# The first stage in one block, and the norm of each stack ahead of its constants

## The chip, the cores and the metric

The kernel runs on one core of a Trainium2 chip. The metric is the device time of one execution in microseconds (us). The kernel before took 4556.93 us, the median of three runs (4550.22 to 4557.34).

A core has five engines with an instruction stream each: TensorE (PE), VectorE (DVE), ScalarE (ACT), GpSimd (POOL) and SyncE (SP). They meet through semaphores. [...]

## What is computed

Input x is 2 x 1024 x 128 in float32. Four parts follow each other, each adding to x what it makes of a normalised x:

```python
x = x + attn_a(layernorm(x))     # 16 heads of 8, causal over 1024 tokens, full softmax
x = x + stack(layernorm(x))      # 6 layers: windowed attention (16 heads of 64, window 32), then a gated FFN;
                                 # ahead of each of the two, half of the features shift by one token
x = x + attn_b(rmsnorm(x))       # gated slot attention, 4 heads of 32, a scan over the tokens
x = x + stack(layernorm(x))      # the same six layers' worth again
```

Only the first part and the entry of the two stacks matter for the change. In the first part q, k and v are projections of the normalised x with a bias, the scores are `q k^T / sqrt(128)` below the diagonal, and the softmax of them weighs v.

## The kernel before

Everything is kept feature-major: `xT` is 128 features by 2048 tokens, cut into NC = 4 chunks of 512 tokens. Each part is one or more blocks. At the end of a block all engines meet, and the next block's instructions begin on all of them together.

*Loading (block 1).* SP loads two identities, the matrix `jmean` and x (1 MB, tokens on the partitions) into `xtok`. TensorE turns it into banks 0 to 3, ScalarE copies the banks into `xT`, VectorE sets three small constants.

*First stage, block 2.* SP loads the four weights and biases and two masks. GpSimd blanks the packing buffers and fills the padded values: `qp`, `kp` (twice, zeros and then rows of ones), `nmz`, `vz`, and counts each in `blank_set`, to 7 (lines 331 to 340). TensorE, ScalarE and VectorE run the layer norm, a chain over the four chunks: product with jmean, centring, square, product with jmean, logarithm, exponential, multiplication (`ln_pe`, `ln_act`, `ln_dve`, lines 111 to 145). When all is normalised (`norm_done`), TensorE transposes the weights, ScalarE copies them into `wT`, and the twelve projections follow, q, k and v of each chunk, through six banks. Since float32 products are made of a high and a low part here, ScalarE copies a projection rounded to its high part (`qhi`, `khi`, line 378), and VectorE makes the low part from the bank (`qlo`, `klo`, line 391); ScalarE copies v into `vz` (line 381). ScalarE waits for `blank_set` 7 ahead of all twelve copies.

*First stage, block 3.* The scores of a pair of heads need their rows packed: the 8 rows of a head are copied by DMA four times under each other (high, low, high, low for q; high, high, low, low for k). That is 16 DMAs of 32 KB for a pair (`pack`, line 409), in six slots. SP issues those of q for all 16 pairs and those of k from pair 3 on; ScalarE those of k for pairs 0 to 2 (EARLY). TensorE then runs through a hand-written order (`turns`, lines up to 300): 12 score pieces of a pair, each reduced to a negative maximum by VectorE (line 571), then the maxima packed in, and from the 15th step on the turned scores with ScalarE's exponentials, GpSimd's masks and the products with the values beside them. The stretch up to the first exponential is called the fill below.

*Stack entry.* SP issues the constants (`rot` of 2 MB, `band`, `head_of`, `take`, `minus_hi`, line 707), four small scales (line 710), and then eight pairs of weights (lines 714 and 717). TensorE waits for all five constants (`const_ld`) and then runs the norm. VectorE waits for GpSimd's zeroing (`zeroed`, lines 791 to 794) and for the constants, copies `take` (line 1063), runs the norm, and copies `y` with the shift into `xs`, two copies a chunk (line 1070). The first step of the loop waits for `take_set`, for the first chunk of `xs` and for the weights of all eight pairs.

Of the kernel before, what the change touches and what calls it, by code (L numbers as in the profile page):

```python
# [5 lines left out]
F32 = mybir.dt.float32  # L6
BF16 = mybir.dt.bfloat16
F32R = mybir.dt.float32r
# [65 lines left out]
def hybrid_kernel(nc, w, c, out):  # L74
# [10 lines left out]
    with ctx:  # L85
# [61 lines left out]

# [6 lines left out]
        with ExitStack() as inner:  # L154
            scope[0] = inner
            xtok = sb("xtok", [P, N // P, D])
            with nc.Block() as block:
                @block.sync
                def _(sp):
                    for n, (dst, src) in enumerate(((ident[:, :], c["ident"]), (identb[:, :], c["identb"]),  # L160
                                                    (jmean[:, :], c["jmean"]))):
                        sp.dma_start(dst, src).then_inc(const_ld, 16)
                    sp.dma_start(xtok[:, :, :], w["L0_attn_a_x"].rearrange("b (n p) d -> p (b n) d", p=P))\
                        .then_inc(x_ld, 16)

                @block.tensor
                def _(pe):
                    pe.wait_ge(const_ld, 48)
                    pe.wait_ge(x_ld, 16)
                    for k in range(NC):  # L170
                        for i in range(4):
                            m = pe.transpose(bank[k][:, i * P:(i + 1) * P], xtok[:, 4 * k + i, :], ident[:, :])
                        m.then_inc(tin_mm, 1)

                @block.scalar
                def _(act):
                    for k in range(NC):
                        act.wait_ge(tin_mm, k + 1)
                        act.activation(xT[:, cs(k)], bank[k][:, :], ACT.Copy).then_inc(tin_cp, 1)

                @block.vector
                def _(dve):
                    dve.memset(ln_eps[:, :], LN_EPS).then_inc(eps_set, 1)
                    dve.memset(ss_eps[:, :], SS_EPS).then_inc(eps_set, 1)
                    dve.memset(ss_back[:, :], SS_BACK).then_inc(eps_set, 1)
            scope[0] = ctx


        stage_a(nc, w, c, sem, bank, wide, xT, y, ident, identb, ln_pe, ln_act, ln_dve, cs, 0, cen, sqr, rstd)
# [39 lines left out]
def stage_a(nc, w, c, sem, bank, wide, xT, y, ident, identb, ln_pe, ln_act, ln_dve, cs, ln_call, cen, sqr, rstd):  # L229

    PP = HA // 2
# [52 lines left out]
    with ExitStack() as st:  # L284
# [24 lines left out]
        norm_done = sem("a_normed")  # L309
# [8 lines left out]

        with nc.Block() as block:
            @block.sync  # L320
            def _(sp):
                for i, nm in enumerate("qkvo"):
                    sp.dma_start(wtok[:, i, :], w[f"L0_attn_a_W{nm}_w"]).then_inc(a_ld, 16)
                    sp.dma_start(bias[:, i:i + 1], w[f"L0_attn_a_W{nm}_b"].rearrange("(p a) -> p a", a=1))\
                        .then_inc(a_ld, 16)
                for dst, src in ((rowm[:, :], c["a_rowm"]), (dmask[:, :], c["a_dmask"])):
                    sp.dma_start(dst, src).then_inc(a_ld, 16)

            @block.gpsimd
            def _(pool):  # L330
                pool.memset(qp[:, :, :].bitcast(F32), 0.0).then_inc(blank_set, 1)
                pool.memset(kp[:, :, :].bitcast(F32), 0.0).then_inc(blank_set, 1)
                pool.wait_ge(blank_set, 2)
                for e in range(2):
                    pool.memset(kp[64 * e + NMAX:64 * e + NLOW + 1, :, :].bitcast(F32), 1.0).then_inc(blank_set, 1)
                    pool.wait_ge(blank_set, 3 + e)
                pool.memset(nmz[:, :, :, :], 0.0).then_inc(blank_set, 1)
                pool.memset(vz[:, :, :, :], 0.0).then_inc(blank_set, 1)
                pool.wait_ge(blank_set, 6)
                pool.memset(vz[:, :, :, VONE:VONE + 1], 1.0).then_inc(blank_set, 1)  # L340

            @block.tensor
            def _(pe):
                ln_pe(pe, ln_call, lambda k: xT[:, cs(k)])
                pe.wait_ge(a_ld, 16 * 10)
                pe.wait_ge(norm_done, 1)
                for i in range(4):
                    m = pe.transpose(bank[0][:, i * P:(i + 1) * P], wtok[:, i, :], ident[:, :])
                m.then_inc(wt_mm, 1)
                pe.wait_ge(wt_cp, 1)  # L350
                for k in range(NC):
                    for i in range(3):
                        n = 3 * k + i
                        o = pbank(n)
                        if n >= 6:
                            if i < 2:
                                pe.wait_ge(lo_cp, 2 * (k - 2) + i + 1)
                            else:
                                pe.wait_ge(v_cp, k - 1)
                        if i < 2:  # L360
                            m = pe.matmul(o, wT[:, i, :], hT(k), start=True, stop=True)
                        else:
                            for t in range(4):
                                m = pe.matmul(o[:, t * P:(t + 1) * P], y[:, (4 * k + t) * P:(4 * k + t + 1) * P],
                                              wT[:, 2, :], start=(t == 0), stop=(t == 3), skip_group_check=True)
                        m.then_inc(pr_mm, 1)

            @block.scalar
            def _(act):
                ln_act(act, ln_call)  # L370
                act.wait_ge(wt_mm, 1)
                act.activation(wT[:, :, :], bank[0][:, :].rearrange("p (i d) -> p i d", i=4), ACT.Copy).then_inc(wt_cp, 1)
                act.wait_ge(blank_set, 7)
                for n in range(3 * NC):
                    k, i = divmod(n, 3)
                    act.wait_ge(pr_mm, n + 1)
                    if i < 2:
                        act.activation((qhi, khi)[i][:, k, :].bitcast(F32R), pbank(n), ACT.Identity, bias=bias[:, i:i + 1])\
                            .then_inc(hi_cp, 1)
                    else:  # L380
                        act.activation(vz[:, 4 * k:4 * k + 4, :, 0:HD],
                                       pbank(n).rearrange("p (t h r) -> p t h r", t=4, r=HD), ACT.Copy).then_inc(v_cp, 1)

            @block.vector
            def _(dve):
                ln_dve(dve, ln_call, lambda k: xT[:, cs(k)], hT)
                dve.drain().then_inc(norm_done, 1)
                for k in range(NC):
                    for i in range(2):
                        dve.wait_ge(hi_cp, 2 * k + i + 1)  # L390
                        dve.scalar_tensor_tensor(out=(qlo, klo)[i][:, k, :].bitcast(F32R), in0=pbank(3 * k + i),
                                                 scalar=bias[:, i:i + 1], in1=(qhi, khi)[i][:, k, :],
                                                 op0=ALU.add, op1=ALU.subtract).then_inc(lo_cp, 1)
# [24 lines left out]
        with nc.Block() as block:  # L418
            @block.sync
            def _(sp):  # L420
                sp.wait_ge(blank_set, 4)
# [13 lines left out]
            def _(pe):  # L435
                def turned_scores(x, e):
# [87 lines left out]
            def _(act):  # L524
                def oz_copy(act, x):
# [8 lines left out]
                act.wait_ge(blank_set, 4)  # L534
                act.wait_ge(lo_cp, 4)
                for p in range(EARLY):
                    pack(act, p, kp, (khi, khi, klo, klo))
# [1389 lines left out]
```

## Time and profile before

| | us |
|---|---|
| median of three runs | 4556.93 |
| lowest, highest | 4550.22, 4557.34 |
| the profiled execution | 4552.66 |
| its span in the trace | 4550.9 |

The profile is one execution. Its first part gives for each engine the busy time, its share of the span and the count of instructions. A row of the busy table by stretch has the window (us from the span's start) and its length, then for PE, PEld (weight loads), DVE, ACT and POOL the busy us with the count in brackets, then the granted clock of TensorE as a share of full speed (1.00 is 2.4 GHz, 0.50 is 1.2 GHz, values between are a mean of the two over the window), then the share of the DMA engines that was busy, and GB/s. A row of the timeline has start, duration, engine, line and operation, output <- input with shapes, a count of merged instructions, and in brackets the idle time of the engine before it and what ended it. SPq and ACTq are the issuing queues; the duration of a DMA there is the time to issue it, not to move its bytes.

### The profile page before, as it was taken

Reading aid. Unit: us, or ns where it says so; the run is one execution under the profiler, and the core shown is the slowest. Engines: PE = TensorE matmul, PEld = TensorE weight load, DVE = VectorE, ACT = ScalarE, POOL = GpSimd, SP = SyncE. Lnnn points to the kernel's source line nnn. Section 1 sums busy time; section 2 is a strip of 40 time slices with the busy share of each in tenths; the row PEclk is TensorE's granted clock in tenths of the full one; section 3 lists DMA queues with packets and bytes.
Section 4 is the critical chain, followed back from the end, with each engine's and each line's share of the span. In section 5 each row is a group of like instructions: output and inputs, shape, how many; then the busy total and the mean of one; then the engine's idle time right before and its main releaser. Section 6 shows DMA issues by size and latency. Waiting matters only on the chain. (4 is left out here: it accounts for less than half of the span.)

```text
span 4550.9 us, 115940 instructions
## 1 busy us (share of the span) xinstructions
PE 4202.9 (92%) x44625; PEld 2515.2 (55%) x44625; DVE 3453.2 (76%) x4977; ACT 3069.5 (67%) x7028; POOL 1809.8 (40%) x1075
## 2 busy tenths in 40 slices
PE   5997999999999999999857579999999999999996
PEld 3443556555656555556526445656556556655653
DVE  4773888888888888888625468888888888888883
ACT  2554777777777777777652257777777777777774
POOL 2111444444444444444314524444444444444442
PEclk7997999999999999999976589999999999999998
DMA  2112444444443444444200044444434444444331
GB/s 41 28 22 63 95 106 99 104 96 97 104 105 88 110 98 100 97 100 97 61 10 3 3 104 107 101 92 105 104 89 104 97 103 103 93 104 105 91 91 36
DMA packets 239314, 382.03 MB, mean 84 GB/s; under 512 B 65636, under 2 KB 128736, under 8 KB 238472
## 3 DMA queue, kind: packets, MB, share of 16 engines
q1 hardware_dynamic: 238344, 373.28, 35.6%
q8 instruction: 386, 6.32, 0.6%
q10 hardware_dynamic: 384, 0.79, 0.1%
q14 instruction: 200, 1.64, 0.1%
HBM read 39.22 MB, written 1.05 MB: 9 GB/s over the span
## 5 line engine op out<-in xcount | busy, mean ns | idle before, releaser
L801 POOL TENSOR_TENSOR b_prob<-b_prob,b_rinv 128x768 f32<-128x768 f32 x384 | 564.2, 1469 | 1897.6 <-DVE b_rinv L1135 1897.6
L807 POOL TENSOR_TENSOR b_prc<-b_prc,b_sws 128x1024 f32<-128x1024 f32 x384 | 905.8, 2359 | 80.6 <-DMA b_sws<-b_prs 80.6
L1050 ACT ACTIVATE b_prob<-ps,b_nmx 128x96 f32<-128x96 f32 x3072 | 748.8, 362 | 0.0
L845 PEld LDWEIGHTS ps<-ident,b_prob 128*128 128x128 f32 x3072 | 378.8, 141 | 416.2 <-issue 300.9
L1076 DVE SCALAR_TENSOR_TENSOR b_prc<-ps,b_qks,b_rot 128x512 f32<-128x512 f32 x768 | 570.3, 743 | 9.6 <-ACT b_sq L1013 8.7
L1078 DVE SCALAR_TENSOR_TENSOR b_prs<-ps,b_qks,b_rot 128x512 f32<-128x512 f32 x768 | 569.1, 741 | 0.0
L1116 DVE TENSOR_TENSOR b_prc<-b_prc,ps 128x512 f32<-128x512 f32 x384 | 263.4, 686 | 386.3 <-PE ps L901 326.4
L1033 ACT ACTIVATE b_oT<-ps 128x512 f32<-128x512 f32 x384 | 226.9, 591 | 359.5 <-PE ps L859 359.5
L845 PE MATMUL ps<-ident,b_prob 128*128 128x128 f32 x3072 | 464.3, 274 | 2.9 <-ACT b_pT L988 2.9
L1089 DVE SCALAR_TENSOR_TENSOR b_rsp<-b_rhi,b_minus_hi,b_rn 128x512 fp32r<-128x512 f32 x192 | 376.9, 1963 | 114.7 <-ACT b_rn L999 114.7
L936 PE MATMUL ps<-b_wqkv,b_xs 128*128 128x128 f32 x3072 | 446.5, 289 | 1.8 <-DVE b_prs L1078 1.6
L988 ACT ACTIVATE b_pT<-ps 128x512 f32<-128x512 f32 x724 | 436.4, 603 | 10.3 <-PE ps L845 10.2
L859 PE MATMUL ps<-b_pT,b_vs 128*64 128x64 f32 x6144 | 436.8, 234 | 0.3
L890 PE MATMUL ps<-b_xs,b_wqkv 128*128 128x512 f32 x768 | 406.0, 610 | 22.4 <-ACT b_va L1038 8.3
L950 PE MATMUL ps<-b_oT,b_wo 128*128 128x512 f32 x768 | 412.4, 619 | 5.6 <-ACT b_oT L1033 5.6
L859 PE MATMUL ps<-b_pT,b_va 128*64 128x64 f32 x6144 | 399.7, 222 | 0.0
L906 PE MATMUL ps<-b_xs,b_wqkv 128*128 128x512 f32 x768 | 397.3, 599 | 0.5
L936 PEld LDWEIGHTS ps<-b_wqkv,b_xs 128*128 128x128 f32 x3072 | 373.3, 192 | 32.6 <-issue 6.9
L1140 DVE TENSOR_REDUCE b_nmx<-ps 128x8 f32<-128x768 f32 x384 | 353.2, 920 | 48.1 <-PE ps L925 47.6
L859 PEld LDWEIGHTS ps<-b_pT,b_vs 128*64 128x64 f32 x6144 | 307.7, 136 | 110.7 <-issue 64.5
L1132 DVE TENSOR_REDUCE b_ssm<-b_prob 128x8 f32<-128x768 f32 x384 | 361.5, 941 | 0.0
L1026 ACT ACTIVATE b_sq<-ps 128x512 f32<-128x512 f32 x384 | 229.4, 597 | 183.3 <-PE ps L906 182.9
(252 smaller groups left out, 7283.8 us busy)
## 6 DMA issues: line engine op xcount, KB each, us to landing
b_sws<-b_prs SPq DMA_DIRECT2D x1536, 128.0 KB, 2.3
b_vs<-b_va SPq DMA_DIRECT2D x768, 128.0 KB, 2.4
b_wqkv<-in_L_ffn_Wqkv SPq DMA_DIRECT2D x96, 192.0 KB, 2.9
b_xs<-y SPq DMA_DIRECT2D x132, 128.0 KB, 2.4
b_wo<-in_L_ffn_Wo SPq DMA_DIRECT2D x96, 64.0 KB, 2.2
b_xs<-y SPq DMA_DIRECT2D x44, 127.8 KB, 2.4
b_rot<-in_rot SPq DMA_DIRECT2D x2, 2048.0 KB, 7.7
b_w<-in_L_ffn_W SPq DMA_DIRECT2D x24, 170.5 KB
```

The costliest lines, as they stand in the source:

```text
L801: pool.tensor_tensor(prob[:, r, :, P - KEYS:P], prob[:, r, :, P - KEYS:P], rinv[:, r % 2, :].rearrange("p (b a) -> p b a", a=1).broadcast_ ...
L807: pool.tensor_tensor(prc[:, r, :, :], prc[:, r, :, :], sws[:, r % 2, :, :], ALU.add)\
L845: t = pe.transpose(bank[6][:, i * P:(i + 1) * P], prob[:, kd, 4 * e + 2 * h + m, :], ident[:, :])
L859: t = pe.matmul(bank[7][es, n * BLK:(n + 1) * BLK], v[:, es], pT[:, h, 2 * e + m, o * BLK:(o + 1) * BLK], start=(n == 0), stop=(n == NB - ...
L890: pe.matmul(bank[0][:, :], W[:, 0, :], X, start=True, stop=True).then_inc(S["q_mm"], 1)
L906: pe.matmul(bank[1][:, :], W[:, 1, :], X, start=True, stop=True).then_inc(S["k_mm"], 1)
L936: m = pe.matmul(bank[0][:, t * P:(t + 1) * P], xs[:, at:at + P], W[:, 2, :], start=(t == 0), stop=(t == 3), skip_group_check=True)
L950: pe.matmul(bank[3][:, :], wo[:, pair(d), :], oT[:, kd % 2, :], start=True, stop=True).then_inc(S["wo_mm"], 1)
L988: act.activation(pT[:, h, :, :], bank[6].rearrange("p (i q) -> p i q", i=4), ACT.Copy)\
L1050: g = act.activation(prob[:, kb, i, P - KEYS:P], wide[0][:, e * CH + m * KEYS:e * CH + (m + 1) * KEYS], ACT.Exp, bias=nmx[:, kb % 2, i:i + 1])
L1076: dve.scalar_tensor_tensor(out=prc[:, r, i, :], in0=bank[i][:, :], scalar=scale, in1=rot[:, 2 * i, t], op0=ALU.mult, op1=ALU.mult)
L1078: dve.scalar_tensor_tensor(out=prs[:, r % 2, i, :], in0=bank[i][:, :], scalar=scale, in1=rot[:, 2 * i + 1, t], op0=ALU.mult, op1=ALU.mult) ...
```

## The change

1. Blocks 1 to 3 become one block. `xtok` is no longer a buffer of its own but a view of `y`. The copies into `xT` and the products with jmean are coupled by `tin_cp` chunk by chunk. GpSimd's blanking stands at the start of its stream.
2. TensorE transposes the weights when the last chunk is centred (`cen_done`), no longer after the last normalised chunk; each chunk's projections wait for that chunk's `norm_done`.
3. On ScalarE only the copy of the first v waits for `blank_set` 7. Its order is: copies of chunks 0 and 1, key DMAs of pair 0, copies of chunks 2 and 3, key DMAs of pairs 1 and 2. Before, all copies came first.
4. TensorE waits for all low parts and all copies of v (`lo_cp`, `v_cp`) ahead of its first score.
5. In a stack TensorE runs the norm ahead of its wait for the constants. VectorE too, and it copies each chunk with the shift right behind that chunk's norm (`each`); the copy of `take` comes behind the norm. SP issues the weights of the first pair (FIRST) ahead of the constants, and the others behind the scales; the first two steps of the loop wait for the first pair's weights alone.

The core of the diff:

```diff
-        def ln_dve(dve, n, src, dst, gain=None):
+        def ln_dve(dve, n, src, dst, gain=None, each=None):
...
+                    if each:
+                        dve.wait_ge(norm_done, NC * n + i + 1)
+                        each(i)
...
+        xtok = y[:, :].rearrange("p (n d) -> p n d", d=D)
...
+        def x_ready(pe, k):
+            pe.wait_ge(tin_cp, k + 1)
...
             @block.tensor
             def _(pe):
-                ln_pe(pe, ln_call, lambda k: xT[:, cs(k)])
+                x_turns(pe)
+                ln_pe(pe, ln_call, lambda k: xT[:, cs(k)], x_ready)
                 pe.wait_ge(a_ld, 16 * 10)
-                pe.wait_ge(norm_done, 1)
+                pe.wait_ge(cen_done, NC)
...
                 for k in range(NC):
+                    pe.wait_ge(norm_done, k + 1)
+                    if k == 1:
+                        pe.wait_ge(lnv_done, NC)
...
+                pe.wait_ge(lo_cp, 2 * NC)
+                pe.wait_ge(v_cp, NC)
...
             @block.scalar
             def _(act):
+                x_copies(act)
+                ln_act(act, ln_call)
...
+                        else:
+                            if k == 0:
+                                act.wait_ge(blank_set, 7)
...
+                def keys(p):
+                    act.wait_ge(lo_cp, 4)
+                    pack(act, p, kp, (khi, khi, klo, klo))
+
+                projections(0)
+                projections(1)
+                keys(0)
+                projections(2)
+                projections(3)
+                for p in range(1, EARLY):
+                    keys(p)
...
+        FIRST = 1
...
+                for p in range(FIRST):
+                    load_qkv(0, p)
+                    load_wo(0, p)
                 for dst, src in ((rot[:, :, :], c["rot"]), (band[:, :, :], c["band"]), (head_of[:, :], c["head_of"]),
...
-                for p in range(PAIRS):
+                sp.wait_ge(S["wqkv_ld"], ONE + 16 * (PAIRS * L0 + FIRST))
+                for p in range(FIRST, PAIRS):
                     load_qkv(0, p)
                     load_wo(0, p)
...
+                ln_pe(pe, ln_call, lambda k: xT[:, cs(k)])
                 pe.wait_ge(S["const_ld"], ONE + 80 * (rep + 1))
-                ln_pe(pe, ln_call, lambda k: xT[:, cs(k)])
                 pe.wait_ge(S["take_set"], ONE + rep + 1)
...
-                            pe.wait_ge(S["wqkv_ld"], ONE + 16 * PAIRS * (L0 + 1))
+                            pe.wait_ge(S["wqkv_ld"], ONE + 16 * (PAIRS * L0 + (FIRST if j < 2 * FIRST else PAIRS)))
...
-                dve.wait_ge(S["zeroed"], ONE + ZERO * (rep + 1))
+                def shift(k, dve=dve):
+                    if k == 0:
+                        dve.wait_ge(S["zeroed"], ONE + ZERO * (rep + 1))
+                    for to, frm in shifted(k):
+                        dve.tensor_copy(to, frm).then_inc(S["xin_done"], 16)
+
+                ln_dve(dve, ln_call, lambda k: xT[:, cs(k)], lambda k: y[:, cs(k)], each=shift)
                 dve.wait_ge(S["const_ld"], ONE + 80 * (rep + 1))
```

## Rows read from the trace of the kernel before

**Rows 1.** The page's first part: busy time, share and instructions of each engine.

```profile
PE 4202.9 (92%) x44625; PEld 2515.2 (55%) x44625; DVE 3453.2 (76%) x4977; ACT 3069.5 (67%) x7028; POOL 1809.8 (40%) x1075
```

**Rows 2.** Busy time by stretch: the fill, and the start of each stack.

```profile
60.00:100.00 40.00, 27.61 (x112) 13.82 (x112) 27.62 (x35) 0.00 (x0) 0.00 (x0) 0.50 0.41 58
...
400.00:405.00 5.00, 0.00 (x0) 0.00 (x0) 0.44 (x1) 1.28 (x1) 0.00 (x0) 0.72 0.65 215
...
2620.00:2625.00 5.00, 2.81 (x6) 0.91 (x4) 2.29 (x4) 1.18 (x1) 1.18 (x5) 0.92 0.12 23
```

**Rows 3.** The timeline from 0 to 54 us, all engines.

```profile
0.90 0.06 DVE L183 MEMSET ln_eps<- 128x1 f32 x1 [0.90 <-PEq L1916]
...
13.59 5.22 POOL L331 MEMSET a_qp<- 128x6144 f32 x1 [13.05 <-POOLq L157]
...
25.44 0.60 ACT L372 ACTIVATE a_wT<-ps 128x512 f32<-128x512 f32 x1 [1.58 <-PE ps L348]
...
32.20 1.05 PE L364 MATMUL ps<-a_wT,y 128*128 128x128 f32 x8
...
43.29 0.52 POOL L340 MEMSET a_vz<- 128x256 f32 x1
43.85 0.69 ACT L378 ACTIVATE cen<-ps,a_bias 128x512 fp32r<-128x512 f32 x1 [17.81 <-POOL a_vz L340]
...
46.62 0.62 ACT L381 ACTIVATE a_vz<-ps 128x512 f32<-128x512 f32 x1
46.88 0.74 DVE L391 SCALAR_TENSOR_TENSOR a_klo<-ps,a_bias,rstd 128x512 fp32r<-128x512 f32 x1
...
53.28 0.75 DVE L391 SCALAR_TENSOR_TENSOR a_klo<-ps,a_bias,rstd 128x512 fp32r<-128x512 f32 x1
```

**Rows 4.** The timeline from 54 to 96 us: key DMAs, first score of pairs 0 to 2.

```profile
54.38 1.90 ACTq L409 DMA_DIRECT2D a_kp<-rstd  x2
...
62.75 2.30 ACTq L409 DMA_DIRECT2D a_kp<-rstd  x2
...
66.69 0.47 PE L477 MATMUL ps<-a_kp,a_qp 64*128 64x128 f32 x2 [13.28 <-DMA a_kp<-a_klo]
...
79.14 0.47 PE L477 MATMUL ps<-a_kp,a_qp 64*128 64x128 f32 x2
...
94.19 0.47 PE L477 MATMUL ps<-a_kp,a_qp 64*128 64x128 f32 x2
```

**Rows 5.** The timeline of the first stack's entry, 400 to 425 us.

```profile
400.72 0.34 SPq L707 DMA_DIRECT2D b_rot<-in_rot  x1
...
407.50 0.13 POOL L794 MEMSET b_xs<- 64x1 f32 x2
...
410.96 3.78 PE L115 MATMUL ps<-xT,jmean 128*128 128x512 f32 x4 [11.84 <-DMA b_minus_hi<-in_minus_hi]
411.00 0.43 DVE L1063 CAST b_take<-b_prs 128x512 fp32r<-128x512 f32 x1 [10.56 <-DMA b_minus_hi<-in_minus_hi]
...
417.76 0.68 DVE L143 TENSOR_TENSOR y<-cen,rstd 128x512 f32<-128x512 f32 x1
...
418.87 0.69 DVE L138 TENSOR_TENSOR cen<-xT,ps 128x512 f32<-128x512 f32 x1 [0.43 <-PE ps L115]
...
422.86 0.69 DVE L143 TENSOR_TENSOR y<-cen,rstd 128x512 f32<-128x512 f32 x1 [0.64 <-ACT rstd L130]
423.64 3.59 DVE L1070 COPY b_xs<-y 64x512 f32<-64x512 f32 x8
...
424.77 2.04 PE L890 MATMUL ps<-b_xs,b_wqkv 128*128 128x512 f32 x2 [3.33 <-DVE b_xs L1070]
```

**Rows 6.** The timeline of the second stack's entry, 2623 to 2648 us.

```profile
2623.80 0.33 SPq L707 DMA_DIRECT2D b_rot<-in_rot  x1
...
2634.17 3.78 PE L115 MATMUL ps<-xT,jmean 128*128 128x512 f32 x4 [11.36 <-DMA b_minus_hi<-in_minus_hi]
...
2647.43 1.33 PE L890 MATMUL ps<-b_xs,b_wqkv 128*128 128x512 f32 x2 [3.34 <-DVE b_xs L1070]
```

More of the change, by code:

```diff
@@ L151, in hybrid_kernel @@
         eps_set = sem("eps_set")
[L154 to L186, printed above, removed]
@@ new lines, in x_copies, with eps_values @@
+        def x_copies(act):
+            for k in range(NC):
+                act.wait_ge(tin_mm, k + 1)
+                act.activation(xT[:, cs(k)], bank[k][:, :], ACT.Copy).then_inc(tin_cp, 1)
+            act.wait_ge(eps_set, 3)
+        def eps_values(dve):
+            dve.memset(ln_eps[:, :], LN_EPS).then_inc(eps_set, 1)
+            dve.memset(ss_eps[:, :], SS_EPS).then_inc(eps_set, 1)
+            dve.memset(ss_back[:, :], SS_BACK).then_inc(eps_set, 1)
+        def x_ready(pe, k):
+            pe.wait_ge(tin_cp, k + 1)
@@ L435, in _ @@
             def _(pe):
+                x_turns(pe)
+                ln_pe(pe, ln_call, lambda k: xT[:, cs(k)], x_ready)
+                pe.wait_ge(a_ld, 16 * 10)
+                pe.wait_ge(cen_done, NC)
+                for i in range(4):
+                    m = pe.transpose(bank[0][:, i * P:(i + 1) * P], wtok[:, i, :], ident[:, :])
+                m.then_inc(wt_mm, 1)
+                pe.wait_ge(wt_cp, 1)
+                for k in range(NC):
+                    pe.wait_ge(norm_done, k + 1)
+                    if k == 1:
+                        pe.wait_ge(lnv_done, NC)
+                    for i in range(3):
+                        n = 3 * k + i
+                        o = pbank(n)
+                        if n >= 6:
+                            if i < 2:
+                                pe.wait_ge(lo_cp, 2 * (k - 2) + i + 1)
+                            else:
+                                pe.wait_ge(v_cp, k - 1)
+                        if i < 2:
+                            m = pe.matmul(o, wT[:, i, :], hT(k), start=True, stop=True)
+                        else:
+                            for t in range(4):
+                                m = pe.matmul(o[:, t * P:(t + 1) * P], y[:, (4 * k + t) * P:(4 * k + t + 1) * P],
+                                              wT[:, 2, :], start=(t == 0), stop=(t == 3), skip_group_check=True)
+                        m.then_inc(pr_mm, 1)
+                pe.wait_ge(lo_cp, 2 * NC)
+                pe.wait_ge(v_cp, NC)
                 def turned_scores(x, e):
@@ L524, in _, with projections @@
             def _(act):
+                x_copies(act)
+                ln_act(act, ln_call)
+                act.wait_ge(wt_mm, 1)
+                act.activation(wT[:, :, :], bank[0][:, :].rearrange("p (i d) -> p i d", i=4), ACT.Copy).then_inc(wt_cp, 1)
+                def projections(k):
+                    for i in range(3):
+                        n = 3 * k + i
+                        act.wait_ge(pr_mm, n + 1)
+                        if i < 2:
+                            act.activation((qhi, khi)[i][:, k, :].bitcast(F32R), pbank(n), ACT.Identity, bias=bias[:, i:i + 1])\
+                                .then_inc(hi_cp, 1)
+                        else:
+                            if k == 0:
+                                act.wait_ge(blank_set, 7)
+                            act.activation(vz[:, 4 * k:4 * k + 4, :, 0:HD],
+                                           pbank(n).rearrange("p (t h r) -> p t h r", t=4, r=HD), ACT.Copy).then_inc(v_cp, 1)
+                def keys(p):
[8 more added lines that the diff above has]
+                    keys(p)
                 def oz_copy(act, x):
@@ L532, in oz_copy @@
                                 act.activation(oz[:, c_, :], bank[3][:, :], ACT.Copy).then_inc(oz_cp, 1)
[L534 to L537, printed above, removed]
                 for x in range(LAST):
@@ L552, in _ @@
             def _(pool):
+                pool.memset(qp[:, :, :].bitcast(F32), 0.0).then_inc(blank_set, 1)
+                pool.memset(kp[:, :, :].bitcast(F32), 0.0).then_inc(blank_set, 1)
+                pool.wait_ge(blank_set, 2)
+                for e in range(2):
+                    pool.memset(kp[64 * e + NMAX:64 * e + NLOW + 1, :, :].bitcast(F32), 1.0).then_inc(blank_set, 1)
+                    pool.wait_ge(blank_set, 3 + e)
+                pool.memset(nmz[:, :, :, :], 0.0).then_inc(blank_set, 1)
+                pool.memset(vz[:, :, :, :], 0.0).then_inc(blank_set, 1)
+                pool.wait_ge(blank_set, 6)
+                pool.memset(vz[:, :, :, VONE:VONE + 1], 1.0).then_inc(blank_set, 1)
                 zero = pool.to_reg(0.0)
@@ L561, in _ @@
             def _(dve):
+                eps_values(dve)
+                ln_dve(dve, ln_call, lambda k: xT[:, cs(k)], hT)
+                for k in range(NC):
+                    for i in range(2):
+                        dve.wait_ge(hi_cp, 2 * k + i + 1)
+                        dve.scalar_tensor_tensor(out=(qlo, klo)[i][:, k, :].bitcast(F32R), in0=pbank(3 * k + i),
+                                                 scalar=bias[:, i:i + 1], in1=(qhi, khi)[i][:, k, :],
+                                                 op0=ALU.add, op1=ALU.subtract).then_inc(lo_cp, 1)
+                dve.wait_ge(blank_set, 7)
                 for g in range(GS):
```

110 lines of the change are left out of this document (29 added, 81 removed).

## The prediction, made before the change was run

> **What bounds the kernel now.** The page's busy shares come first: TensorE is busy for 92% of the span [rows 1]. A change that leaves TensorE's work alone can therefore only gain where TensorE stands still, so the next view is the table of busy time by stretch. The change touches no line inside the long loops of the two stacks, so the stretches to look at are the front of the first stage and the two stack entries: from 60 to 100 us TensorE has 27.61 us of work in 40 us, at a granted clock of 0.50, and ScalarE has none [rows 2]. The timeline of these places is read third, and the reader is to look at the bracket behind each row: it says what ended the idle time.
>
> In the first stage two waits follow each other. GpSimd starts its blanking memsets only when the second block starts, at 13.59, and ends them at 43.81 (43.29 + 0.52), a run of 30.2 us; ScalarE's copies of the projections wait 17.81 us for that [rows 3]. When the last low part is made (53.28 + 0.75 = 54.03), a block ends, and the packing DMAs begin at 54.38. The first score waits for them until 66.69, idle for 13.28 us [rows 3, 4]. At each stack entry the norm, which needs nothing but xT, waits for the constants: the block starts at 400.72 and the first mean product at 410.96; in the second stack it is 2623.80 and 2634.17, and from there to the first projection 13.8 and 13.3 us pass [rows 5, 6].
>
> **The first stage, part by part.** *Blanking.* The memsets move to the start of the program. The other engines' first instructions stand at 0.90 there [rows 3], so the run ends at 0.9 + 30.2 = 31.1. No memset is added. GpSimd's later masks are far behind (their first exponentials come after the fill), so nothing waits behind the move.
>
> *Projections of chunks 0 and 1.* In the trace of before the last product of chunk 1 ends at 32.20 + 1.05 = 33.25 [rows 3]. The weight transposes now don't wait for the last norm but for the last centred chunk, so at least the 1.58 us go that ScalarE stood idle before its copy of the weights at 25.44 [rows 3]: 31.7 at most. q0 and k0 are copied under the memsets. The copy of v0 keeps its wait and starts at 31.1. Copies started back to back come every 0.57 us (six from 43.85 to 47.24, rows 3): q1 at 31.7, k1 at 32.3, v1 at 32.85, ended at 33.5. VectorE's low part of k1 starts 0.83 us after its copy (46.88 against 46.05, which is 46.62 less one step) and takes 0.74: 33.85 [rows 3]. Then both queues may pack pair 0, at 33.9 instead of 54.38: 20.5 us earlier.
>
> *Pair 0 and the projections of chunks 2 and 3.* This is the new order, and the one place where the change adds a wait. ScalarE's queue issues the 8 key DMAs of pair 0 first, and these took from 54.38 to 62.75, 8.4 us (1.05 us each) [rows 4]. Behind them on ScalarE stand the six copies of chunks 2 and 3; behind these the lower parts on VectorE; and TensorE now waits for all of those ahead of its first score. ScalarE is free at 33.9 + 8.4 = 42.3, the fifth copy (k3) starts at 42.3 + 4 x 0.57 = 44.6, its low part ends 0.83 + 0.75 later at 46.2. The other arm is the landing: from the start of packing to the first score it took 66.69 - 54.38 = 12.3 us [rows 4], which gives 33.9 + 12.3 = 46.2. Both arms end together, and the first score starts at about 46.2 instead of 66.69: **-20.5 us**. Whichever arm is late costs one for one. TensorE's own products for chunks 2 and 3 run beside ScalarE's issuing from 32 on and hide.
>
> *Pairs 1 and 2.* Before, the keys of pair 1 were issued from 62.75 and the first score of pair 1 stood at 79.14, 12.4 us behind the first of pair 0 [rows 4]. Now they are issued from 45.7, take 8.4, and land 3.9 later (66.69 against 62.75, rows 4), at 58.0. They are wanted at 46.2 + 12.4 = 58.6, so 0.6 us are to spare. Pair 2 is issued until 62.5, lands at 66.4, and is wanted at 94.19 - 20.5 = 73.7 [rows 4]. SP's own packing begins 20.5 us earlier like everything else and keeps its lead. The fill is a chain of products and reductions that does not change, so the 20.5 us arrive at the stage's end. Bounds: -22 if landing and copies both come a little early; if an issue came a third dearer, at 1.4 us instead of 1.05, 2.8 us would be lost in each of pairs 0 and 1, less the 0.6 to spare, so -15.5.
>
> The Trainium skill ("DMA: Bandwidth & Descriptors", Issuing engines are not separate DMA queues) says that DMAs of ScalarE and SP run on the same 16 engines and interleave, and that a second issuer saves only issue time. By that rule a pause of ScalarE's issuing lets SP run ahead and loses no transfer time, and pair 1 would land earlier than I count; no run here shows it yet.
>
> **The stack entries.** The first mean product needs only xT and may start with the block, at about 400.95. That moves the norm by 10.0 us. From its first mean product to the last normalised chunk it took 410.96 to 423.55 [rows 5]. Into VectorE's part of it come the shift copies, 3.59 us for eight, or 0.9 us for a chunk [rows 5]. Chunk 0: y at 407.76, ended 408.44, copies to 409.4. GpSimd's zeroing, for which they wait, ends at 407.50 + 0.13, just in time. The fourth centring stood at 418.87, would be at 408.87, and comes at 409.4, so 0.55 us late, and the last y with it: 422.86 - 10.0 + 0.55 = 413.4. It ends at 414.1, its copies at 415.0. Then the copy of take, which was ahead of the norm and is now behind it, 0.43 us [rows 5]: 415.45. The first projection starts at 415.5 instead of 424.77: **-9.3 us**.
>
> Of the queue: SP issues the first weights ahead of the constants, two more DMAs, and its remaining 14 behind the scales as before. The constants landed 10.2 us after the block's start (410.96, rows 5); with a tenth more bytes ahead of them (by the shapes 256 KB, beside 2 MB of rot and 0.5 MB of the others) and two more issues that becomes some 11.5 to 12, against the 14.7 us at which they are now wanted. I cost it at nothing; the cover is 3 us. The weights of the other pairs are wanted by the third slot only.
>
> The clock: a stack's block starts with a granted clock that is not yet at its lower level (0.72 over 400 to 405, 0.92 over 2620 to 2625, rows 2), while the norm of before started at the lower one. The first four records of mean products took 3.78 us at the lower one [rows 5]; at twice the clock some 1 us of that goes ahead of the first centring. In stack 0 the zeroing at 407.63 holds the copies, which caps the gain at -10.0. In stack 1 nothing does: up to -10.5. I take **-9.7** and **-10.0**; the ends are -9.3 and -10.0, and -9.4 and -10.5. The loops behind are unchanged and start earlier by as much.
>
> **The sum.** 20.5 + 9.7 + 10.0 = 40.2 us. The profiled execution took 4552.66, so its like would take 4512.5; the median of the three runs is 4556.93, and two of them stand at 4557, which gives 4516.7. I predict **4515**. Terms at their ends give -34 to -43.
>
> **The rivals.** *Late keys* (A): ScalarE's issuing is slower than before or pair 1 lands late, because SP competes for the whole time. For it: the two arms are level and only 0.6 us are to spare. Against: SP competed before too. It gives back 5 to 10 us: about 4523.
>
> *Constants bind again* (B): they land after 14.7 us, or the early weights delay them, and the norm's lead turns into a new wait on the same constants. Half of the stacks' 19.7 is lost: about 4525. It is also the form in which the change wouldn't do what it says.
>
> *Warm fill* (C): the fill of before ran wholly at 0.50 [rows 2], after 13.28 us of idle TensorE [rows 4]; now the idle stretch in front is some 8 us. Were it warm, TensorE's 27.61 us there would be about half, and since VectorE's reductions (27.62 us of these 40, rows 2) are then the limit, some 5 us more go: about 4510. The Trainium skill ("TensorE: Matmul & The Clock Gate", What's actually happening) says that the low clock is the default and that activity releases it; by that rule the fill, unchanged in density, stays cold and C fails.
>
> *Slower* (D): ScalarE issues become much dearer, since the keys now sit between its copies. Price with 3.6 us an issue: the first score at 33.9 + 28.8 + 3.9 = 66.6, pair 1 at 33.9 + 28.8 + 3.4 + 28.8 + 3.9 = 98.8, pair 2 at 127.6, where it was wanted at 94.19 before [rows 4]. That is 33 us late less 19.7 from the stacks: 4570. It decides from some 3.3 us an issue on, and the trace shows 1.05 [rows 4].
>
> **How the numbers follow.** Forecast (-34 to -43) 0.60; A 0.15; B 0.09; C 0.08; D 0.03; the shift is absorbed later, within 9 us of no change, 0.04; left over 0.01. The range reaches over A, B and C and takes in the 7 us between the runs shown: 4504 to 4532. Chances: faster by over 0.2% (about what a measurement of this kernel can tell from no change, 9 us) 0.93, same 0.04, slower 0.03.
>
> **What would show it.** After: the last blanking memset ends near 31; ScalarE's first key DMA at 34; first score at 46, released by a DMA or by VectorE's last low part; pair 1's first score without a wait for a DMA; in each stack the first mean product with the block's first instructions and the first projection 14.5 to 15 us later, released by VectorE's copy of take. A wait of the take copy for minus_hi would be B, a wait of pair 1's score for a DMA would be A. The prediction is wrong if the fill is longer than 34 us or if the loops' own pace changes.

## The result and the profile after

| | before | after |
|---|---|---|
| median of four runs | 4557.14 | 4510.53 |
| lowest, highest | 4550.22, 4560.46 | 4507.91, 4520.66 |
| the profiled execution | 4552.66 | 4512.50 |

The ratio is 0.991, with a 95% interval of 0.9894 to 0.9926: 34 to 48 us less. The forecast was 4515, in a range of 4504 to 4532. Between the two profiled executions lie 40.2 us, which is what the sum gave; between the medians lie 46.6. Single runs of one kernel here differ by ten us and more, so both agree with the sum.

The front of the changed kernel, in the timeline (start, duration, engine, line, operation, in brackets the idle time before it and its releaser):

```profile
0.83 5.22 POOL L541 MEMSET a_qp<- 128x6144 f32 x1 [0.29 <-POOLq L1933]
...
30.53 0.53 POOL L550 MEMSET a_vz<- 128x256 f32 x1
31.16 0.60 ACT L502 ACTIVATE a_vz<-ps 128x512 f32<-128x512 f32 x1 [4.52 <-PE ps L389]
...
33.80 1.90 ACTq L333 DMA_DIRECT2D a_kp<-rstd  x2
...
42.18 0.69 ACT L497 ACTIVATE cen<-ps,a_bias 128x512 fp32r<-128x512 f32 x1 [8.78 <-issue]
42.35 1.07 ACTq L333 DMA_DIRECT2D a_kp<-rstd  x1
...
45.21 0.74 DVE L566 SCALAR_TENSOR_TENSOR a_klo<-ps,a_bias,rstd 128x512 fp32r<-128x512 f32 x1
...
46.01 0.48 PE L439 MATMUL ps<-a_kp,a_qp 64*128 64x128 f32 x2 [9.90 <-DVE a_klo L566]
```

These answer to [rows 3, 4]. The blanking runs from 0.83 to 31.06 and not from 13.59 to 43.81. The copy of v0 starts when the blanking ends, although the bracket names the product, which had long been done. Packing starts at 33.80 (before: 54.38), and the first score at 46.01 (before: 66.69), 20.7 us earlier. Its bracket now names VectorE's last low part and not a DMA. The DMAs were hardly ahead of it: the last count on the semaphore of pair 0, which says that its 16 DMAs have landed, comes at 45.79 in this trace, and the low part ended at 45.95.

The entry of the first stack, same view, against [rows 5]:

```profile
382.89 0.64 SPq L717 DMA_DIRECT2D b_wqkv<-in_L_ffn_Wqkv  x1
...
382.93 3.44 PE L115 MATMUL ps<-xT,jmean 128*128 128x512 f32 x4 [1.65 <-PEq L342]
...
389.67 0.13 POOL L809 MEMSET b_xs<- 64x1 f32 x2
...
389.93 0.87 DVE L1080 COPY b_xs<-y 64x512 f32<-64x512 f32 x2 [0.20 <-POOL b_xs L809]
...
396.86 0.43 DVE L1084 CAST b_take<-b_prs 128x512 fp32r<-128x512 f32 x1
...
397.39 2.05 PE L905 MATMUL ps<-b_xs,b_wqkv 128*128 128x512 f32 x2 [4.02 <-issue]
...
400.11 0.55 SPq L717 DMA_DIRECT2D b_wqkv<-in_L_ffn_Wqkv  x1
```

The mean product starts with the block. VectorE's take copy has no bracket: it waited for nothing, so the constants had landed. The last count on their semaphore comes 11.5 us behind the start of either block. The first projection follows the take copy within 0.1 us, 14.5 us behind the block's start (before: 24.05). In the second stack it is 13.4 (2607.39 against 2593.96) and was 23.6 [rows 6]. The weights of the eighth pair are issued only behind the first projection, at 400.11.

The lead of the changed kernel over the one before, from the two timelines. A mark is the start of an instruction that both kernels have; "loops done" is VectorE's last addition to xT behind the loops.

| mark | before | after | lead |
|---|---|---|---|
| first score | 66.69 | 46.01 | 20.7 |
| first exponential | 101.13 | 80.14 | 21.0 |
| first stage's last instruction | 399.15 | 381.32 | 17.8 |
| first projection, stack 0 | 424.77 | 397.39 | 27.4 |
| stack 0's loops done | 2319.2 | 2288.9 | 30.3 |
| first projection, stack 1 | 2647.43 | 2607.39 | 40.0 |
| stack 1's loops done | 4542.7 | 4502.5 | 40.2 |

Three steps make it: 20.7, 9.6 and 10.2 us, in all 40.4. Between them 3.2 us are lost behind the fill and 2.9 gained in the first stack's loops, where nothing was changed. The experiments had to say whether these two belong to the change.

### The profile page after: what moved, and what is told of

Read it like the earlier page. It is cut to its first block and busy times, and to the rows that moved or that the text cites. A ratio compares the mean times of both kernels' runs of the same rounds, so it can differ in the third digit from the quotient of the medians.

```text
span 4510.8 us, 115928 instructions
## 1 busy us (share of the span) xinstructions
PE 4195.9 (93%) x44625; PEld 2511.7 (56%) x44625; DVE 3451.3 (77%) x4977; ACT 3074.1 (68%) x7028; POOL 1811.6 (40%) x1075
## 5 line engine op out<-in xcount | busy, mean ns | idle before, releaser
L1003 ACT ACTIVATE b_pT<-ps 128x512 f32<-128x512 f32 x724 | 436.3, 603 | 14.6 <-PE ps L860 11.1
L905 PE MATMUL ps<-b_xs,b_wqkv 128*128 128x512 f32 x768 | 405.6, 610 | 22.1 <-issue 14.6
L874 PEld LDWEIGHTS ps<-b_pT,b_vs 128*64 128x64 f32 x6144 | 307.7, 136 | 110.9 <-issue 64.5
```

What stands on the lines that cost most here:

```text
L874: t = pe.matmul(bank[7][es, n * BLK:(n + 1) * BLK], v[:, es], pT[:, h, 2 * e + m, o * BLK:(o + 1) * BLK], start=(n == 0), stop=(n == NB - ...
L905: pe.matmul(bank[0][:, :], W[:, 0, :], X, start=True, stop=True).then_inc(S["q_mm"], 1)
L1003: act.activation(pT[:, h, :, :], bank[6].rearrange("p (i q) -> p i q", i=4), ACT.Copy)\
```

## The experiments

The times of a group stand beside runs of the kernel before on the same chip. The theory: the three steps add up and are all there is. The rivals: a part of the lead is given back, or more is gained, behind the marks; or something other than the named wait brings a step.

**The two halves alone.** The first kernel has the changed first stage and the stacks of before:

```diff
-def stack(rep, ...):      # changed
+def stack(rep, ...):      # before
```

> The changed first stage with the stacks of the kernel before. Theory: the two parts add up, and this one is worth the 20.7 us by which the first score came earlier: the time is 18 to 21 us below the kernel before (ratio near 0.9956). The fill ends 21 us earlier, the stack's block starts 18 to 21 us earlier. Rival: the first stage's lead is given back behind the fill (the trace of the changed kernel showed a lead of 17.8 us at the stage's end); then the stack's block starts no more than 18 us earlier, here too. Second rival: the changed kernel's 46.6 us by the medians are more than its parts, since the loops run at another pace; then this run gains clearly more than 21 us.

The second has the first stage of before and the changed stacks, with `each` in `ln_dve`:

```diff
-def stack(rep, ...):      # before
+def stack(rep, ...):      # changed
```

> The first stage of the kernel before with the changed stacks. Theory: each entry is worth 9.6 and 10.2 us, in all 19 to 20 us below the kernel before (ratio near 0.9957), and first projections 14.5 and 13.4 us behind their block's start. Rival: something behind the entries moves too; then the sum of the two halves is not the whole and this run gains clearly more or less than 20.

Measured: ratio 0.9955 (0.9940 to 0.9971) for the first, 0.9945 (0.9930 to 0.9959) for the second, or 20 and 25 us. The product is 0.990, that of the whole is 0.990 to 0.991. The marks are where they were in the whole: first score 46.0 in the first kernel, first projections 14.49 and 13.45 us behind their blocks in the second. The lead at the first stage's end was 21.2 us in the first kernel and not 17.8, so the 3.2 us are not given back by the changed first stage as such. The halves add up within their intervals. The medians can't say more than that.

**The blanking held back.** Everything as in the changed kernel, but GpSimd waits for the first centred chunk:

```diff
             def _(pool):
+                pool.wait_ge(cen_done, 1)
                 pool.memset(qp[:, :, :].bitcast(F32), 0.0).then_inc(blank_set, 1)
```

> The changed kernel, but GpSimd's blanking waits for the first centred chunk, so it starts near 15.0 instead of 0.83. The theory that the end of the blanking sets when packing may start: first key DMA at 33.8 + 14.1 = 47.9, first score at 60.1, and the time some 14 us above the changed kernel. The rival, that merging the blocks and the earlier weight transposes bring the lead: first score below 50, and the time within 3 us of the changed kernel.

The first score came at 60.2, and ScalarE's wait is back in the timeline:

```profile
45.16 0.60 ACT L502 ACTIVATE a_vz<-ps 128x512 f32<-128x512 f32 x1 [18.73 <-POOL a_vz L551]
...
60.22 0.47 PE L439 MATMUL ps<-a_kp,a_qp 64*128 64x128 f32 x2 [9.17 <-DMA a_kp<-a_klo]
```

The ratio was 0.9934 (0.9912 to 0.9957). That is 11 us above the changed kernel's 0.9910, or 15 above the 0.9900 of its second comparison below, with an interval of ten us either way; the mark says it better. So 14.2 of the 20.7 us are the early start of the blanking. The other 6.5 lie behind its end: there packing starts 2.7 us later (45.07 to 47.81), where it took 10.6 before (43.81 to 54.38), while the blanking itself ended 1.3 us later than before. Only four copies are left there, since q0 and k0 are copied under the blanking and packing no longer stands behind a block's end, that is behind chunks 2 and 3. The earlier transposes have no visible part in it: in the changed kernel the products of chunk 1 end at 29.40, and the first copy of chunk 1 starts, behind the blanking, at 31.65. What the new order does is asked below.

**The weights last.** In the stacks the weights are issued behind constants and scales, and the first step waits for all eight pairs, as before; the norm stays early:

```diff
-                for p in range(FIRST):
-                    load_qkv(0, p)
-                    load_wo(0, p)
...
-                sp.wait_ge(S["wqkv_ld"], ONE + 16 * (PAIRS * L0 + FIRST))
-                for p in range(FIRST, PAIRS):
+                for p in range(PAIRS):
...
-                            pe.wait_ge(S["wqkv_ld"], ONE + 16 * (PAIRS * L0 + (FIRST if j < 2 * FIRST else PAIRS)))
+                            pe.wait_ge(S["wqkv_ld"], ONE + 16 * (PAIRS * L0 + PAIRS))
```

> The changed kernel, but in the stacks the weights are issued in the order of before, all behind the constants and scales, and the first step waits for all eight pairs. Theory: the last pair is issued 17.7 us behind the block's start and lands 2 to 3 us later, so the first projection starts at 20 to 21 us instead of 14.5 and 13.4, and each stack loses 6 to 7 us: 12 to 14 us above the changed kernel. Rival: the norm's early start alone brings the gain, the weights were never due: the first projection stays at 14.5 and the time within 2 us of the changed kernel.

The first projections started 19.6 us behind both blocks, 5.1 and 6.1 us late. In the timeline of the first stack the last weights that the projection waits for are issued at 399.26, and it follows:

```profile
399.26 0.55 SPq L717 DMA_DIRECT2D b_wqkv<-in_L_ffn_Wqkv  x1
...
402.35 2.04 PE L901 MATMUL ps<-b_xs,b_wqkv 128*128 128x512 f32 x2 [8.96 <-issue]
```

The bracket names no DMA, but the last count on the weights' semaphore comes 19.4 us behind each block, 0.2 ahead of the projection. The kernel changes two things, the order and the wait, and the trace of the changed kernel tells them apart: there the last of the eight pairs lands 20.1 and 19.9 us behind the block, so with the old wait the new order would be no better. More than half of the 9.6 and 10.2 us is had only because the first step no longer waits for all weights. Whether the first pair has to be issued first is not tested by itself. Here, issued behind the constants, the first 16 counts of the weights' semaphore, as many as one DMA gives, were there 11.3 us behind the block, well ahead of 14.5 and 13.4, so its place probably does not matter.

The ratio was 0.9951 (0.9932 to 0.9970), 19 to 23 us above the changed kernel's two ratios where the marks explain 11; each ratio is uncertain by 7 to 9 us. In the one profile the second stack's loops took long. From VectorE's first product to the start of the last additions to xT it was 1901.0 us, where most kernels here have 1887 to 1894. The old order of weights is not needed for that: the last kernel below has the changed order and took 1897.8.

**The copies first.** ScalarE's order of before in the changed kernel:

```diff
-                projections(0)
-                projections(1)
-                keys(0)
-                projections(2)
-                projections(3)
-                for p in range(1, EARLY):
+                for k in range(NC):
+                    projections(k)
+                for p in range(EARLY):
                     keys(p)
```

> The changed kernel with ScalarE's order of before: all twelve copies, then the keys of pairs 0, 1, 2. The prediction's theory, that two arms are level and ScalarE's issuing is a closed stretch: the key DMAs slip by the six copies, 3.4 us, to 37.2, and the first score comes 3.4 us later, at 49.4. Rival, from the trace of the changed kernel, where the products of chunks 2 and 3 were done at 36.1 and ScalarE's sequencer had already gone on to DMAs while the copies ran: the key DMAs start at 36.2, the first score at 48.4 or a little earlier, 2 to 2.4 us late. In neither does the run's time move by more than its spread.

Both theories were wrong on the first score, and the rival right on the key DMAs (ratio 0.9903, 0.9879 to 0.9926, which tells nothing here). The key DMAs start 2.3 us later, while SP issues from 33.85 as before, and the first score comes 1.1 us earlier, at 44.88:

```profile
36.15 2.06 ACTq L333 DMA_DIRECT2D a_kp<-rstd  x2
...
44.88 0.47 PE L439 MATMUL ps<-a_kp,a_qp 64*128 64x128 f32 x2 [8.77 <-DMA a_kp<-a_klo]
```

An arm is one of the two chains that the first score waits for, copies with low parts on one side, the landing of the DMAs on the other. The low parts are made at 37.1, so only the landing arm is left. In this order it is shorter than in the trace of before: the eight issues take 6.5 us (36.15 to 42.65) and not 8.4, and the score starts 2.2 us behind them and not 3.9.

In the order of the change the landing arm is as long as it was before. Three kernels with that order show it by the bracket of the first score:

```profile
46.15 0.48 PE L439 MATMUL ps<-a_kp,a_qp 64*128 64x128 f32 x2 [10.03 <-DMA a_kp<-a_klo]
```

This is the kernel with the weights last, whose front is that of the changed kernel and whose key DMAs start at 33.81. With the blanking held back the DMA released the score too, 12.4 us behind the first key DMA, and with the late waits for take, below, at 45.90. In the changed kernel the landing came at 45.79, 12.0 us behind. So both arms end within 0.2 us of each other, and the new order on ScalarE brings nothing in this kernel; by the one profile of the other order it costs a microsecond. Why eight issues are faster when SP is already four ahead is not settled.

**Two steps further.** In one kernel, GpSimd blanks `vz` first, and each consumer waits for its own part:

```diff
-                pool.memset(qp[:, :, :].bitcast(F32), 0.0).then_inc(blank_set, 1)
...
+                pool.memset(vz[:, :, :, :], 0.0).then_inc(blank_set, 1)
+                pool.wait_ge(blank_set, 1)
+                pool.memset(vz[:, :, :, VONE:VONE + 1], 1.0).then_inc(blank_set, 1)
+                pool.memset(qp[:, :, :].bitcast(F32), 0.0).then_inc(blank_set, 1)
...
-                                act.wait_ge(blank_set, 7)
+                                act.wait_ge(blank_set, 2)
...
-                sp.wait_ge(blank_set, 4)
+                sp.wait_ge(blank_set, 6)
```

> The changed kernel with the blanking in another order: vz and its ones first, then qp, kp and the rows of ones, nmz last; each consumer waits for what it needs. Theory, that the end of the blanking binds: the copy of v0 need no longer wait, the rows of ones end at 0.8 + 28.4 = 29.2, the fourth low part is made at about 29.7, key DMAs at 29.7 instead of 33.8, first score at 42.0 instead of 46.0, and 4 us off the time. Rival, that the projections bind: the first score stays within 1 us of 46.0.

Key DMAs at 29.4, first score at 41.6: 4.4 us earlier, as the first theory has it. The ratio was 0.9889 (0.9874 to 0.9905).

In the other, TensorE's waits for the constants and for take move to the first instructions that need them:

```diff
                 ln_pe(pe, ln_call, lambda k: xT[:, cs(k)])
-                pe.wait_ge(S["const_ld"], ONE + 80 * (rep + 1))
-                pe.wait_ge(S["take_set"], ONE + rep + 1)
...
                 def strips(U, b, pe=pe):
+                    if not b:
+                        pe.wait_ge(S["const_ld"], ONE + 80 * (rep + 1))
...
                         UB, kb = um(b)
+                        if isinstance(b[0], int) and b[0] == 0 and b[1] == 0:
+                            pe.wait_ge(S["take_set"], ONE + rep + 1)
```

> The changed kernel, but TensorE waits for the constants at its first strip of sums and for take where it first uses it, not ahead of its first step. Theory, that VectorE's chain with the take copy at its end sets the first step: TensorE's first projection starts at 8 to 9 us behind the block instead of 14.5 and 13.4, but the first product on VectorE only at 14.4 and 13.5 instead of 17.3 and 16.2, so each stack gains 2.8 us, 5.7 in all. Rival: TensorE's early start brings the full 6 us each, 12 in all. Second rival: the constants' landing takes the place (first strip), and less than 2 us come in all.

The projections started at 10.5 and 9.3 us, but VectorE's first products at 14.68 and 13.43 instead of 17.31 and 16.25: 2.6 and 2.8 us, the first theory. VectorE's chain is what a stack's entry now waits for. The ratio was 0.9902 (0.9887 to 0.9917), which does not resolve 5.4 us.

Both together:

> e6 and e7 together. Theory: the gains add, 4 + 5.7 = 9.7 us below the changed kernel, so some 50 to 56 us below the kernel before (ratio near 0.9885). Rival: one hides behind the other; then no more than 6 us below the changed kernel.

First score 41.5, first products 14.49 and 13.43. The ratio was only 0.9898 (0.9881 to 0.9915), with single runs from 4490 to 4515. The marks and the times did not agree, so the changed kernel and this one were run once more, side by side, with a third:

> The changed kernel once more, for a second profile and more times. Theory, that its lead over the kernel before is the three early starts (20.7, 9.6 and 10.2 us) and all beyond is the spread of single runs: the same marks again (key DMAs at 33.8, first score at 46.0, first projections 14.5 and 13.4 us behind their blocks), and a lead of 38 to 48 us, while the stretches between the marks (first stage behind the fill 296 to 302 us, third part 296 to 304 us, loops 1891 to 1906 us) differ from the first profile by some us either way. Rival, that the loops or the third part are truly shorter in the changed kernel: the sum of these stretches is again lower than in the kernel before by more than 5 us.

> vz first and take late once more, on the same chip as the changed kernel. Theory: the marks stay (first score 41.5, first products 14.5 and 13.4 us behind the blocks), 4.5 + 2.8 + 2.8 = 10.1 us less than the changed kernel by the marks, and its median is lower by 5 to 15 us. Rival, that what is won at these places is lost behind them: the median is within 4 us of the changed kernel's.

The changed kernel gave 4507.81 (ratio 0.9900, 0.9883 to 0.9916), the version with both 4494.21 (0.9876, 0.9860 to 0.9893), 13.6 us less where the marks say 10: by the medians of this comparison it is the fastest kernel here, though the intervals overlap and the first comparison had it level with its two halves. Its marks were the same again (41.3; 14.49 and 13.43), and so were those of the changed kernel (33.8; 46.0; 14.6 and 13.4). The stretches between the marks were not: the first stage behind the fill took 307.7 us in this profile of the changed kernel, after 301.2 in the first, and 298.1 in the kernel before; that is more than the 296 to 302 that I expected. The rival that the changed stacks have shorter loops falls: from the first projection to the end of the first stack's loops it is 1891.5 and 1891.7 us in the two profiles of the changed kernel and 1894.4 in the one before, but 1891.0 in the kernel with the old stacks behind the changed first stage, and 1894.4 and 1897.8 in two with the new stacks, the weights last and the copies first. Nor is anything gained or lost in the sum: the four stretches between the marks (first stage behind the fill, both stacks' loops, third part) add up to 4391.4 us before and to 4391.9 in both profiles of the changed kernel.

The last one copies chunk 2 ahead of the keys of pair 0, on top of both:

```diff
                 projections(1)
-                keys(0)
                 projections(2)
+                keys(0)
                 projections(3)
```

> As e10, but ScalarE copies chunk 2 before it issues the keys of pair 0; only chunk 3 comes behind them. In e6 the products of chunk 2 were done at 31.3, two us after the key DMAs began. Theory, that the longer arm is now key issuing plus the six copies: the key DMAs start 2 us later, at 31.3, but are faster since SP is ahead of them (8 in 6.5 us rather than 8.4, as in e5), and only three copies follow: low parts done at 39.9, first score at 40.1 to 40.9 instead of 41.5. Rival: the landing binds, first score at 41.5 or later. The time can't tell them apart, the marks can.

The first score came at 40.10, released by the low part, 1.2 to 1.5 us earlier, with key issues from 31.74 to 37.87, 6.1 us for eight. The mark goes the way of the theory; the time, 4498.19 (0.9884, 0.9868 to 0.9901), can't show it.

**Where the spread of single runs sits.** The same instructions, in stretches without any change, from the first exponential to the stage's end. Columns as in the table of busy time by stretch: busy us of PE, PEld, DVE, ACT and POOL with their counts, then the granted clock. The kernel before, and under it its third part:

```profile
101.10:399.20 298.10, 270.12 (x1894) 122.36 (x1892) 190.01 (x257) 168.48 (x400) 40.60 (x64) 0.94 0.14 21
...
2319.20:2622.80 303.60, 194.94 (x5333) 156.35 (x5333) 140.35 (x263) 110.33 (x177) 114.99 (x168) 0.65 0.02 6
```

The changed kernel's first profile:

```profile
80.10:381.30 301.20, 272.85 (x1896) 123.49 (x1892) 190.09 (x256) 168.69 (x400) 40.77 (x64) 0.92 0.14 21
```

Its second profile:

```profile
80.40:388.10 307.70, 280.54 (x1896) 125.44 (x1892) 190.18 (x256) 168.86 (x400) 40.59 (x64) 0.89 0.14 21
```

The kernel with the copies first:

```profile
79.30:374.70 295.40, 267.03 (x1894) 121.53 (x1892) 190.17 (x256) 168.79 (x400) 40.60 (x64) 0.95 0.14 20
```

The third part in the kernel with the changed stacks alone:

```profile
2304.90:2601.40 296.50, 189.25 (x5333) 153.14 (x5333) 140.22 (x264) 110.54 (x177) 114.60 (x168) 0.68 0.02 6
```

In the four rows of the first stage VectorE's and ScalarE's busy times are the same to 0.4 us, and TensorE's go with the length: 295.4 us at a mean granted clock of 0.95, 298.1 at 0.94, 301.2 at 0.92, 307.7 at 0.89. The third part, the gated slot attention between the stacks, which no run changed, is 7 us longer at 0.65 than at 0.68. Together the two stretches took 594.5 us in the kernel with the changed stacks alone and 608.2 in the second profile of the changed kernel: 13.7 us between two executions, in code that is the same in both. What made the clock differ is not shown.

## Why the prediction was right, step by step

- *Blanking ends at 31.1*: 31.06. *Packing starts at 33.9*: 33.80. *First score at 46.2*: 46.01, so 20.7 us for 20.5. Holding the blanking back moved all three by 14.
- *Two level arms*: both were right. The arm of issuing and copies ended at 45.95 (said: 46.2). The landing came at 45.79, 12.0 us behind the start of packing (said: 12.3). Which one releases the score changes from profile to profile. What the prediction did not ask is what the order of before would give: with the copies first the landing arm shrinks to 8.7 us (36.15 to 44.88), and the score comes 1.1 us earlier. The new order was not needed.
- *ScalarE's issuing as a closed stretch, pair 1 issued from 45.7 with 0.6 us to spare*: wrong. The keys of pair 1 were issued from 42.35, beside the copies of chunks 2 and 3 (42.18 to 45.6): the queue went on once the copies had been handed to the engine. Pair 1's first score stood at 58.45 without a wait (said: 58.6), and its 16 DMAs had landed at 54.3. The spare time was 4.1 us and not 0.6, so A had less to stand on than I gave it.
- *The fill as long as before*: 34.13 us (46.01 to 80.14) against 34.44. The granted clock was 0.50 but for one stretch; 65 to 70 us in the first and in the second profile of the changed kernel:

```profile
65.00:70.00 5.00, 2.79 (x16) 1.36 (x14) 4.43 (x6) 0.00 (x0) 0.00 (x0) 0.84 0.33 48
...
65.00:70.00 5.00, 3.23 (x16) 1.56 (x14) 4.24 (x5) 0.00 (x0) 0.00 (x0) 0.50 0.31 47
```

In the second profile the whole fill ran at 0.50 and took 34.45 us. The other kernels bear it out: six profiles with a fill wholly at 0.50 have 34.44 or 34.45 us, seven with some full clock in it 33.7 to 34.1. So C fell nearly whole, and the one stretch at full clock gave back 0.3 us, where C counted some 5 for a fill that is warm throughout. By the Trainium skill's rule that activity releases the low clock ("TensorE: Matmul & The Clock Gate", What's actually happening) it would stay cold at the same density. The trace agrees for most of the fill (0.55 in the mean of the first profile, 0.50 in the second) and not for all of it. The recorded sign "wrong if the fill is longer than 34 us" was set too tight: the fill of before was already 34.4.
- *Stack entries, 9.7 and 10.0*: 9.6 and 10.2. GpSimd's zeroing did hold the first shift copy in stack 0 (bracket of 0.20 at 389.93) and did not in stack 1. B fell: the constants landed 11.5 us behind both blocks (said: 11.5 to 12), and take was copied with no wait, 14.0 and 12.9 us behind them. So the cover was 2.5 us in stack 0 and 1.4 in stack 1, where I gave 3.
- *"I cost it at nothing"*, of the weights: right for the change as it stands, but the cover was named too narrowly. What hid the weights was the shorter wait of the first step. With the wait for all pairs the entry would have lost 5.1 and 6.1 us.
- *The sum*: 40.2 for 40.4 by the marks and 40.2 between the profiled executions. That the profiled execution met the forecast for it to 0.1 us is luck: 3.2 us were lost in the first stage behind the fill and 2.9 gained in the first stack's loops, in code that did not change. The 46.6 between the medians lie within the interval of 34 to 48; the second comparison gave 42.4. No run shows a cause in the change for more than its three steps.
- D: eight issues took 8.3 us as before, 1.04 us each, far from the 3.3 us each from which it decides.

## What to carry to other kernels

Read a start-up for the engine that idles before it has anything to wait for, as GpSimd did for 13 us here, and start its work with the program; then order that work by who needs it first, which moved the first score by another 4.4 us. When a wait for one transfer goes, list everything that the same instruction or the first step behind it still waits for: here more than half of the stacks' gain hung on a second wait, that for the weights. And where a gain is small beside the spread, measure it at marks in the timeline, such as the first score: in kernels with the same front they repeated to 0.3 us where the run times moved by ten and more.

## What was not expected of the hardware

- ScalarE's queue issued DMAs while its engine still worked through copies that stood ahead of them in the program (DMA at 42.35, copies until 45.57). Copies that stood behind DMAs in the program did wait for all eight issues (none between 33.80 and 42.18).
- Eight DMA issues on ScalarE took 8.0 to 8.4 us when both queues began together, 6.5 when SP was four DMAs ahead, and 6.1 in the last kernel, where it was three ahead, with the same transfers. The cause is open.
- The same stretch of the first stage took 295 to 308 us, in step with its mean granted clock of 0.95 to 0.89.
